# Two more buffer places for the slot experts' weights, in tensors that lie idle between two attentions

## The reference, cut to what matters

```python
q = slot_query                                   # 16 slots, 128 wide
o = q + _mha(q, x, x, d_Wq, d_Wk, d_Wv, d_Wo)    # slots look at the tokens
h = _layernorm(o, e_ln_g, e_ln_b)                # one slot for each of 16 experts
u = silu(einsum('besd,edf->besf', h, e_W1) + e_b1)
g = silu(einsum('besd,edf->besf', h, e_Wg) + e_bg)
y = einsum('besf,efd->besd', u * g, e_W2) + e_b2
o = o + y
out = _mha(x, o, o, c_Wq, c_Wk, c_Wv, c_Wo)      # tokens look at the slots ("CB")
```

## Time and profile before

| | us |
|---|---|
| three runs | 679.38, 673.80, 674.53 |
| median | 674.53 |
| profiled execution, its own time | 679.38 |
| span of the profiled execution | 677.6 |
| mean granted TensorE clock | 0.806 |

### The profile page before, as it was taken

How to read it: one execution, slowest core, us unless ns; L and a number is a source line. 1 busy time by engine, 2 the same in 40 slices (tenths; PEclk the granted TensorE clock), 3 DMA queues, 4 the chain that set the end, 5 groups by cost and what they waited for, 6 DMA issues and landing times.

```text
span 677.6 us, 8699 instructions
## 1 busy us (share of the span) xinstructions
PE 503.5 (74%) x3053; PEld 382.0 (56%) x3053; DVE 347.2 (51%) x1135; ACT 219.0 (32%) x423; POOL 258.3 (38%) x372
## 2 busy tenths in 40 slices
PE   4596992469578756696863049999369967999997
PEld 3443482448365342443762039999134365999997
DVE  4589249731387642179874023442476875333333
ACT  3531823004144510141420006332054244344441
POOL 5831858352337001254337752556364060000000
PEclk9798895559766988698555559999569957899999
DMA  9998500010440008730001121211530000000002
GB/s 289 311 165 190 206 1 0 20 43 15 151 161 1 0 31 218 211 100 0 1 5 51 50 74 51 72 58 32 161 96 0 1 1 0 1 1 1 1 1 62
DMA packets 64107, 48.06 MB, mean 71 GB/s; under 512 B 6441, under 2 KB 55877, under 8 KB 63936
## 3 DMA queue, kind: packets, MB, share of 16 engines
q1 hardware_dynamic: 60560, 41.88, 23.1%
q0 software_dynamic: 3072, 5.06, 2.3%
q10 hardware_dynamic: 432, 0.57, 0.3%
HBM read 35.08 MB, written 13.68 MB: 72 GB/s over the span
## 4 chain that ended last, share of the span: by engine, by line
PE 57%; DVE 19%; POOL 9%; issue 6%; DMA 4%; ACT 3%; SPq 1%; POOLq 0%; ACTq 0%; DVEq 0%
PE ps L1025 9%; PE ps L987 6%; POOL tok L1874 5%; DVE st L1326 4%; PE ps L920 4%; PE ps L922 3%; PE ps L921 3%; DVE rz L1413 3%; PE ps L606 3%; PE ps L717 3%; PE ps L618 2%; PE ps L650 2%; PE ps L660 2%; PE ps L783 2%; DVE x L1633 2%
## 5 line engine op out<-in xcount | busy, mean ns | idle before, releaser
L1947 POOL DMA_INDIRECT res<-qT,dest x48 | 46.7, 974 | 60.8 <-DVE qT L1625 52.9
L1650 DVE SCALAR_TENSOR_TENSOR x<-ps,gate,x 128x128 f32<-128x128 f32 x128 | 36.0, 344 | 62.8 <-PE ps L1025 62.8
L1025 PEld LDWEIGHTS ps<-moe_w,big 128*128 128x128 f32 x512 | 63.2, 196 | 4.2 <-issue 1.8
L1025 PE MATMUL ps<-moe_w,big 128*128 128x128 f32 x512 | 63.6, 280 | 0.3 <-DVE x L1641 0.3
L1251 ACT ACTIVATE big<-ps,col 128x512 f32<-128x512 f32 x64 | 44.0, 688 | 58.8 <-PE ps L922 58.4
L1874 POOL DMA_INDIRECT tok<-r,to_slot x48 | 47.4, 987 | 31.8 <-DVE to_slot L1487 18.4
L916 PE MATMUL ps<-tri,ones 128*128 128x512 bf16 x46 | 18.4, 582 | 53.2 <-DMA tok<-r,to_slot 36.3
L1786 POOL TENSOR_SCALAR rstd<-mv 128x4 f32<-128x4 f32 x44 | 10.5, 238 | 123.1 <-DVE mv L1329 122.1
L1201 ACT ACTIVATE xn<-x,negmean,rstd 128x128 f32<-128x128 f32 x48 | 21.1, 485 | 91.2 <-POOL negmean L1791 91.2
L606 PE MATMUL ps<-con,xn 128*128 128x128 f32 x128 | 31.2, 391 | 25.9 <-DVE xn L1342 20.2
L1789 POOL TENSOR_TENSOR rstd<-rstd,half 128x4 f32<-128x4 f32 x44 | 46.0, 1046 | 0.0
(11 more groups left out here) (285 smaller groups left out, 1151.0 us busy)
## 6 DMA issues: line engine op xcount, KB each, us to landing
ring<-in_ew SPq DMA_DIRECT2D x21, 256.0 KB, 5.3
moe_w<-in_m0w SPq DMA_DIRECT2D x16, 256.0 KB, 6.0
moe_w<-in_m2w SPq DMA_DIRECT2D x16, 256.0 KB, 5.7
big<-res SPq DMA_DIRECT2D x12, 256.0 KB, 4.4
moe_w<-in_ew SPq DMA_DIRECT2D x11, 256.0 KB, 5.3
tok<-zero SPq DMA_DIRECT2D x1, 2580.0 KB, 28.0
big<-tok SPq DMA_DIRECT2D x8, 322.5 KB, 3.0
ring<-in_ewg SPq DMA_DIRECT2D x9, 256.0 KB, 4.9
```

What stands on the lines that cost most here:

```text
L1025: last = mm(ps[7 - i % 2][:, cols(c)], big[:, f, i % B, cols(c)], w[:, e, F + P * f:F + P * f + P], start=f == 0, stop=f == FC - 1)
L1650: last = v.scalar_tensor_tensor(out=x[:, C * t + c, :], in0=ps[7 - i % 2][:, cols(c)], scalar=gate[:, C * t + c, e:e + 1], in1=x[:, C * t ...
L1947: g_.indirect_dma_start(out=res_d[name], out_offset=bass.IndirectOffsetOnAxis(ap=dest[:, at:at + 1], axis=0), in_=ysb[:, i % 2, cols(b)], ...
```

## The change

SLOT_BUFS becomes 12. Place 10 is kv (three units: 30, 31 and 32), place 11 is kr_w (two units: 33 and 34) and rz (one: 35). `slot_w`, which gave a whole place, becomes `slot_unit`, which gives the 512 columns of one unit. kr_w is a float32 name for the memory of kr, whose own name now stands for the same bytes in the rounded type. Steps 10 and 11 are thus loaded right after 5 to 9, and steps 12 to 15 use the places 0 to 3, all of them in ring; they wait for ey_use from 1 to 4 where before steps 10 to 15 waited for 1 to 6.

```diff
-        SLOT_BUFS = 10
+        SLOT_BUFS = 12
...
-        kr = sb("kr", [P, NL0], F32R)
+        kr = under("kr", [P, NL0])
+        kr_w = sb("kr_w", [P, NL0])
...
-        def slot_w(q):
-
-            i = q % SLOT_BUFS
-            return ring[:, i, :] if i < RING else moe_w[:, :, :].rearrange("p a b -> p (a b)")[:, 1536 * (i - RING):1536 * (i - RING + 1)]
+        def slot_unit(j):
+
+            i, at = j // 3 % SLOT_BUFS, slice(512 * (j % 3), 512 * (j % 3) + 512)
+            if i < RING:
+                return ring[:, i, at]
+            if i < 2 * RING:
+                return moe_w[:, :, :].rearrange("p a b -> p (a b)")[:, 1536 * (i - RING):1536 * (i - RING + 1)][:, at]
+            if i == 2 * RING:
+                return kv[:, at]
+            return kr_w[:, at] if j % 3 < 2 else rz[:, :]
...
-                    w = slot_w(q)[:, 512 * (j % 3):512 * (j % 3) + 512]
+                    w = slot_unit(j)
...
-                    return slot_w(q)[:, 512 * (j % 3):512 * (j % 3) + 512]
+                    return slot_unit(j)
```

## The result

| | runs | median us | range |
|---|---|---|---|
| before | 20 | 678.88 | 673.28 to 681.15, one at 1194.58 |
| changed | 20 | 673.01 | 671.16 to 674.46 |

A forecast was written before the change was run, and what follows sets the result against it. The last late weight loads were taken to bound the end of the slot experts. Second products ending at 274.11 instead of 278.35 us gain 4.2, other effects priced at nothing: 674.53 - 4.2 = 670.3 us, range 665.0 to 675.0.

The forecast's parts named there:

- three cases forecast: Whole kernel's time: within 1% of before 76%, faster by over 1% 20%, slower by over 1% 4%.
- The base: Starting time of the whole kernel: median 674.53 us of three runs (673.8 to 679.38), from which the gain was taken.
- The late burst: Late weight loads for the slot experts' second products: six fewer save 5.2 us, the last landing at about 271.1 us.
- the sum over the groups: Four groups of second products in the slot experts: they end at 274.11 instead of 278.35 us, gaining 4.2 us.
- bounds of 2.1 and 5.7: Gain in us at the second products if all four groups run at half clock, or all at full clock.
- Six loads earlier: Loads moved behind the fifteen after the first mixture: no cost, at most 0.02 us, as nobody waits there.
- What is late next: Small steps behind the last group of second products: they move as a block, with no further gain.
- The rival of the early clock: Behind the second products: full clock up to 289.7 us gives 4.4 us more, 8.6 in all, 665.9 us; chance 18%.
- half the gain or none: Second products wholly at half clock (gain 2.1 us) and a later stage's clock worse, or no faster burst: 672.4 us; 16%.
- Slower: Scores and probabilities of the next attention at half clock, 16.7 us more: 687 us; chance 4%.

The follow-up runs named there:

- e5: The changed kernel run again unaltered, beside three others on the same chip; 676.20 us, ratio 0.9908 to the kernel before.
- e4: The changed kernel with SLOT_BUFS = 11, so three units instead of six go early and 15 loads stay late; 678.51 us, ratio 0.9927 to the kernel before.
- e1: The kernel before with six more early loads that nobody reads, all 18 late loads kept; 684.89 us, ratio 1.0001.
- e7: The kernel before with dummy matmuls keeping TensorE busy in the slot experts' waits, including those for late loads; 681.02 us, ratio 0.9978.
- e3: The kernel before with 2, 4 and 4 dummy matmuls ahead of the load waits of groups 2, 3 and 4; 682.00 us, ratio 0.9961.
- e6: The changed kernel with dummy matmuls ahead of the slot experts' remaining waits; 675.99 us, ratio 0.9882 to the kernel before.
- e8: The changed kernel with one dummy matmul ahead of each wait between the second products and the projection; 676.14 us, ratio 0.9905 to the kernel before.
- e2: The changed kernel with 24 late loads instead of 12, the added ones read by nobody; 689.17 us, ratio 1.0073 to the kernel before.

## Why the prediction was right or wrong

**The time.** 673.0 was measured and 670.3 forecast. The gain was forecast at 4.2 us and is 4.3 by the ratio, 5.9 by the medians, 6.2 by the spans, 6.6 in e5 (682.77 - 676.20). That the ratio's 4.3 meets the 4.2 is luck: it averages over 6.6 us against one group of the runs before and 0.8 against the other, and the profile adds its gain up from other terms than the prediction. In all of these the change is below 1%, the likeliest of the three cases forecast, though outside the noise of so many runs.

**The base: a step that failed.** The last step of the sum, 674.53 - 4.2, took a gain that was read from an execution of 679.38 us, one of the longer group, off the median of three runs of which two fell in the shorter group. Twenty runs have a median of 678.88, and 678.88 - 4.2 is 674.7. So the base made the forecast 4.35 us too low, and the gain, too small by 1.7, took part of it back.

**The late burst and the sum over the groups: right in the mechanism.** The second products were to go from 10.0 to 5.8 us (268.32 to 274.11) and took 5.91, no wait for a load in between. The last load was forecast for 271.1, which is 270.3 with the stage 0.83 us earlier, and the DMA engines were done by 270. In e4 load 15 landed 16.3 us after the first late issue (259.88 to 276.15), 15.5 being expected. What the sum didn't have is that the first products' own length now counts. In the kernel before, the last load sets the end of the second products at 22.83 us behind the start of the first (23.07 in e1, 22.64 in e7), and a late group 1 is covered: in e3 it starts 14.23 us behind the first products, and the end is at 22.96 all the same. In the changed kernel TensorE sets it: 20.13 us in the first profile, where group 1 started 14.20 us behind the first products, and 18.03 in e5, with 12.60. So the loads brought 2.7 us in the one and 4.8 in the other. Both are within the bounds of 2.1 and 5.7.

**Six loads earlier: right as far as can be measured.** No cost in e1, and between 193 and 199 us VectorE's instructions take the same time in both profiles (L1342 344 ns, as L1349 in the changed kernel; L1390 425 ns, as L1397). The queue was issued by 194.2 and not by 192, and the DMA engines were mostly done by 198.5, as forecast (share 0.18 from 198.5 to 199, 0.01 behind 200).

**"What is late next": the other step that failed.** The prediction let everything behind group 4 "move as a block". It did move, and it also ran faster: 1.27 us less to the projection and 1.01 less from there to the first reciprocal, 2.3 us in the profile, which the sum put at nothing. This comes back in e5, e6 and e8 (4.2 to 4.3 and 13.9). It is the clock and not another part of the change: e7 has it (4.19 and 13.87) with all late loads in place and TensorE kept busy, and e2 lacks it (5.53 and 14.82), which is the changed kernel with its waits for loads back; so does e1. In e3, with the waits filled, and in e4, with one wait left, part of it is there (4.90 and 14.53, 4.26 and 14.39).

**The rival of the early clock** was right in its mechanism, and the rule of the Trainium skill ("TensorE: Matmul & The Clock Gate", section "HAM oscillation — how this bites in real kernels") that DMA waits between bursts of products throw the clock back agrees with the traces: 1.00 behind the products instead of 0.50. The waits of the page's example are longer, about 3 to 5 us; here they were 0.78 to 1.54 us. I had held against the rival that the small gaps of 0.74, 1.08 and 0.83 us would stay and keep the clock at half; they stayed, and the clock was full. Its price was mis-sized: I halved all of TensorE's 8.7 us for 4.4 and got 2.3, because GpSimd's 2.37 and ScalarE's 1.06 us (L1905 and L1208 of before) became the chain as soon as TensorE was faster.

One reading in the prediction was wrong: that the clock fell after the waits before groups 3 and 4. Ahead of group 3 it rose (0.93 over 272 to 274), and group 3 ran at full clock; it fell once, in the wait before group 4. In the kernel before:

```profile
275.00:275.50 0.50, 0.08 (x4) 0.00 (x0) 0.00 (x0) 0.00 (x0) 0.00 (x0) 1.00 0.19 55
275.50:276.00 0.50, 0.00 (x0) 0.00 (x0) 0.00 (x0) 0.00 (x0) 0.00 (x0) 0.69 0.04 11
276.00:276.50 0.50, 0.13 (x4) 0.14 (x8) 0.00 (x0) 0.00 (x0) 0.00 (x0) 0.50 0.00 0
```

**The other rivals.** The time measured, 673.0, lies nearest to the 672.4 of "half the gain or none", but by the base and not by its mechanism: the groups did not run wholly at half clock (0.62 in the mean from 268.9 to 274.8), and no later stage took longer. "Slower" did not happen; the stretch that this case named ran at 1.00 from 282.5 to 306.

**What stays open.** Why the kernel before has two groups of times on the first chip, and why the change brings only 0.8 us against the shorter one, when the loads alone are worth 4.3 or more in e7 against e6. The clock is the candidate. On the two other chips four of 32 and four of 17 runs of the kernel before are under 680 us, and their mean granted clocks are 0.809 to 0.814, while the median of the other runs is 0.805 and 0.802. But no profile of a short run of the kernel before was taken, so it is argued and not shown in which stage they gain. Nor is it known why the first products run at half clock for longer in some executions than in others (12.6 to 14.2 us to the second products).

## What to carry to other kernels

A wait for loads between bursts of matmuls can cost twice: its length, and the clock of what stands behind it. When such a wait goes, price the dependent matmuls behind it once at half and once at full clock, and then look for the engine that takes the chain over when TensorE gets faster: it caps the gain. Once the loads no longer set the end, a delay of the engine ahead of them, which the wait used to cover, counts in full. And loads can go ahead of time into any tensor that lies idle between two phases, at no cost that was measured here, if the DMA engines are idle there; the first three of the six brought most of it (e4). Take the base of a forecast from enough runs, and from the same group of times as the profile that the gain is read from.

## What was not expected of the hardware

That the same small gaps go with either level of the clock. In the kernel before, with gaps of 0.78, 1.54 and 1.29 us between groups of 1.1 to 2.0 us, the clock was 0.50 behind them; with 5.9 us of unbroken products and then gaps of 0.75, 1.08, 0.83 and 1.42 us it was 1.00, and so it was in e5. Unbroken products just ahead don't secure it, though: in e3 TensorE ran 8.7 us without a break from 270.5 to 279.2, the same gaps of 0.73, 1.08 and 0.83 us followed, and the projection was at half clock again (3.75 us for its first four records). What decides between the two is not shown. And ten dummy matmuls in e3, which compute nothing, brought the kernel before 2.7 us by the ratio (0.4%, with an interval of 0.2 to 0.6%), of which its profile shows 1.0.
